# Local attention: score products over whole images, sorted into strips by TensorE

## The reference

```python
patches = extract_patches(x)                  # 25 shifts, 5x5, zero padding of 2
p = patches.reshape(N, NHEADS, hdim, K2, H, W)
q = x.reshape(N, NHEADS, hdim, 1, H, W)
scores = (p * q).sum(axis=2, keepdims=True)
att = jax.nn.softmax(scores, axis=3)
out = (p * att).sum(axis=3).reshape(N, D, H, W)
out = jnp.einsum('ndhw,od->nohw', out, w_out) + b_out[None, :, None, None]
```

## Time and profile before

| | us |
|---|---|
| median of three runs | 1821.26 |
| profiled execution | 1828.49 |
| its span | 1826.7 |
| PE / DVE / POOL / ACT busy | 1461.7 / 1532.3 / 1187.1 / 1052.0 |
| first half (window attention) | to about 799 |
| score products of head 0 on DVE | 819.4 to 883.3 |
| first subtraction of head 0, of head 7 | 888.6, 1647.3 |
| stores of the last halves | 1739.0 to 1753.7 |

### The profile page before, as it was taken

The page is one execution under the profiler, slowest core; times in us unless marked ns, Lnnn a source line. Parts: engine busy times, 40 slices in busy tenths (PEclk is TensorE's granted clock), DMA queues, the critical chain, the costliest instruction groups (busy, mean ns, idle before and its releaser), DMA issues.

```text
span 1826.7 us, 54921 instructions
## 1 busy us (share of the span) xinstructions
PE 1461.7 (80%) x22057; PEld 766.9 (42%) x22057; DVE 1532.3 (84%) x2231; ACT 1052.0 (58%) x1883; POOL 1187.1 (65%) x860
## 2 busy tenths in 40 slices
PE   5889999999999999946667877769687786867745
PEld 3667777777777777730122221212222122213322
DVE  5987777777777777769999999999989999896924
ACT  3567776666677777645454836667474665544300
POOL 4435554455444555410789899999999999996600
PEclk9999999999999999977789899999989999998878
DMA  8702010202014202032222225241332522117069
GB/s 331 271 14 53 18 53 18 53 18 53 13 48 81 53 18 53 18 108 60 61 50 70 59 50 127 50 110 32 72 92 50 126 50 50 26 44 278 21 266 403
DMA packets 106857, 156.07 MB, mean 85 GB/s; under 512 B 71362, under 2 KB 83650, under 8 KB 100034
## 3 DMA queue, kind: packets, MB, share of 16 engines
q1 hardware_dynamic: 106690, 153.60, 29.1%
HBM read 81.92 MB, written 65.20 MB: 81 GB/s over the span
## 4 chain that ended last, share of the span: by engine, by line
PE 37%; POOL 24%; DVE 18%; issue 13%; ACT 4%; SPq 1%; DVEq 1%; DMA 1%; POOLq 0%; ACTq 0%
POOL arena L801 18%; PE PS L1321 8%; PE PS L1309 6%; PE PS L1445 5%; PE PS L1275 4%; POOL arena L812 4%; PE PS L1300 4%; DVE arena L1213 3%; DVE arena L1104 3%; PE PS L1468 2%; DVE arena L1100 2%; PE PS L1279 2%; DVE consts L1152 2%; PE PS L1393 2%; DVE arena L1186 2%
## 5 line engine op out<-in xcount | busy, mean ns | idle before, releaser
L801 POOL TENSOR_TENSOR arena<-arena 128x2016 f32<-128x2016 f32 (+2 forms) x168 | 605.9, 3658 | 85.6 <-PE PS L1393 85.6
L1213 DVE TENSOR_TENSOR arena<-arena,PS 128x1568 f32<-128x1568 f32 x348 | 610.1, 1778 | 37.3 <-PE PS L1445 31.7
L1445 PE MATMUL PS<-arena,consts 32*32 32x392 f32 x12800 | 390.6, 512 | 101.5 <-DVE arena L1213 66.8
L767 POOL TENSOR_TENSOR arena<-arena,consts 128x196 f32<-128x196 f32 x512 | 294.7, 612 | 159.7 <-ACT arena L851 159.7
L992 ACT ACTIVATE PS<-arena 128x392 f32<-128x392 f32 x348 | 173.0, 499 | 281.9 <-DVE arena L1213 279.5
L1393 PE MATMUL PS<-arena,consts 128*32 128x504 f32 (+2 forms) x1664 | 222.7, 610 | 111.5 <-POOL arena L801 65.2
L1445 PEld LDWEIGHTS PS<-arena,consts 32*32 32x32 f32 x12800 | 137.5, 104 | 356.8 <-DVE arena L1213 206.0
L1321 PE MATMUL PS<-arena 128*128 128x96 f32 x2048 | 265.0, 272 | 3.5 <-ACT arena L864 2.0
L1321 PEld LDWEIGHTS PS<-arena 128*128 128x128 f32 x2048 | 249.1, 192 | 6.1 <-issue 3.9
L774 POOL TENSOR_TENSOR arena<-arena 128x392 f32 (+1 forms) x64 | 78.4, 1225 | 254.5 <-DVE arena L1131 254.5
L876 ACT ACTIVATE arena<-PS 128x512 f32<-128x512 f32 x256 | 151.8, 593 | 105.5 <-PE PS L1309 105.5
(11 more groups left out here) (105 smaller groups left out, 1693.5 us busy)
## 6 DMA issues: line engine op xcount, KB each, us to landing
arena<-x_wide_dram SPq DMA_DIRECT2D x256, 82.5 KB, 2.1
arena<-x_wide_dram SPq DMA_DIRECT2D x32, 660.0 KB, 8.1
x_wide_dram<-arena SPq DMA_DIRECT2D x12, 1125.0 KB
arena<-in_x_dram SPq DMA_DIRECT2D x8, 1568.0 KB, 14.9
x_wide_dram<-arena SPq DMA_DIRECT2D x64, 196.0 KB, 4.8
x_dram<-arena SPq DMA_DIRECT2D x8, 1568.0 KB, 7.7
attn_dram<-arena SPq DMA_DIRECT2D x256, 49.0 KB, 3.0
arena<-x_dram SPq DMA_DIRECT2D x8, 1568.0 KB, 18.1
```

The costliest lines, as they stand in the source:

```text
L767: i = nc.gpsimd.tensor_tensor(k_bd[k][:, r], keys.unsqueeze(1).to_broadcast([P, HEADS_T, S]), head_mask.unsqueeze(2).to_broadcast([P, HEAD ...
L801: nc.gpsimd.tensor_tensor(tile, x_part, by, ALU.mult).then_inc(pool_tile, 1)
L1213: nc.vector.tensor_tensor(by_channel(v_tiles[n % V_RING]), shifted_values(half, k), over_channels(PS[:, 2 + n % W_BANKS, 0:PIX]), ALU.mult ...
L1445: mm = nc.tensor.matmul(PS[dst, 4 + i, 0:PIX], ident[src, src], tile[src, c * PIX:(c + 1) * PIX], start=done == 0, stop=done == NK - 1)
```

## The change

- **Pixels for scores by whole images.** Two buffers `xs_maps` of 56 + 2 rows replace the four. A partition holds one channel of one image (8 channels x 16 images = 128), so one tile covers four strips of all images, `a` being odd or even strips. Products start at the strip's own rows: each row is multiplied once, and every tile has 4 x 7 x 56 = 1568 columns. The two rows below an image are zero.
- **Strips sorted by TensorE.** With a selection of 0 and 1 at stride 2 (`images`), `sum_scores` puts the sum of a strip on its partition, at columns from dy x 56 on. Its last dy rows go also to the next strip's partition, at columns from 0: up to four more matmuls of dy x 56 columns. Strip partitions are now numbered two per image within a group of 32 (`value_sel`, `load_for_values`, `store_half`).
- **DMAs.** The score loads of a head become 4 (were 32), those of its values 64 (were 4), its stores 64 (were 32).
- **Buffers and shares.** Rings of four instead of three (`S_RING`, `V_RING`); eight value products of a head on POOL instead of five; other places for reciprocal and scales.
- **Normalising.** Four steps of 784 pixels for a head's scores, and no clearing of halo rows for them. Small selections are made by POOL and DVE, and the parameters of the score channels by a product and a reduction instead of sixteen copies.

```diff
-TILE = CH * (GR + R) * W
+GROUPS = 4
+TILE = GROUPS * PIX
-S_RING, V_RING = 3, 3
+S_RING, V_RING = 4, 4
-RECIPROCAL_AT = 24
-SCALE_AT = [1, 3]
-SHARE_AT = [[9, 13], [18, 21, 24]]
-POOL_SHARE = [[(16, 18), (17, 21, 22)]] * (LH - 1) + [[range(18, NK), range(15, NK)]]
+RECIPROCAL_AT = 23
+SCALE_AT = [2, 4]
+SHARE_AT = [[8, 10, 12, 14], [17, 19, 21, 23]]
+POOL_SHARE = [[(11, 13, 16, 18), (13, 17, 21, 22)]] * (LH - 1) + [[range(18, NK), range(15, NK)]]
...
-                add("pe", ("sum", ("score", j, t, a)), 0.2 + 1.67e-3 * rows * cols,
+                add("pe", ("sum", ("score", j, t, a)), 0.85 + (0.1 + 0.095 * t_dy(t) if t_dy(t) else 0),
...
-        xs_halves = [room(GROUPS * HALO).rearrange("p (g h w) -> p g h w", g=GROUPS, h=HR) for _ in range(4)]
+        xs_maps = [room(IMAGE + R * WP).rearrange("p (h w) -> p h w", w=WP) for _ in range(2)]
         sc = [room(NK * PIX).rearrange("p (k n) -> p k n", k=NK)]
         early_pairs = used[1] // HW
...
-            r0, rows = R - dy, GR + dy
-            X = xs_halves[s_buf(j, a)]
-            here, there = X[:, :, r0:r0 + rows, R:R + W], X[:, :, R:R + rows, R + dx:R + dx + W]
+            X = xs_maps[j % 2]
+            def strips(down, right):
+                first = X[:, GR * a + down, R + right:R + right + 1]
+                return bass.AP(first.tensor, first.offset, [list(first.ap[0]), [2 * GR * WP, GROUPS], [WP, GR], [1, W]])
+            here, there = strips(0, 0), strips(dy, dx)
...
-            def load_for_scores(j, a, g, loaded):
-                for c in range(CH):
-                    src = bass.AP(at.tensor, at.offset, [[STRIP, GROUP], [1, HALO]])
+            def load_for_scores(j, half, loaded):
+                for b2 in range(2):
+                    src = bass.AP(at.tensor, at.offset, [[LINE, HD], [IMAGE, Q], [1, IMAGE]])
...
             def load_for_values(j, a):
-                for b2 in range(2):
-                    src = bass.AP(at.tensor, at.offset, [[STRIP, C], [LINE, CH], [1, HALO]])
+                for i in range(GROUPS):
+                    for b2 in range(2):
+                        for c in range(CH):
+                            src = bass.AP(at.tensor, at.offset, [[IMAGE, BP], [STRIP, 2], [1, HALO]])
...
                 for i in range(GROUPS):
                     for c in range(CH):
-                        sp.dma_start(dst[first:first + GROUP], o_loc[half][c * GROUP:(c + 1) * GROUP, i]).then_inc(o_stored[half], 16)
+                        for b2 in range(2):
+                            dst = attn_dram[b2, j * HD + half * CH + c, :, 2 * i:2 * i + 2]
+                            first = c * GROUP + b2 * 2 * BP
+                            src = o_loc[half][first:first + 2 * BP, i]
+                            sp.dma_start(dst, src).then_inc(o_stored[half], 16)
...
+            nc.vector.tensor_reduce(fold, ident.rearrange("p (c r) -> p r c", c=GROUPS), AX_X, ALU.add)
...
             for u in range(UNITS - 3, UNITS):
                 dve.wait_ge(added, u + 1)
                 unit_stats(u)
...
-            for g in range(GROUPS):
-                for c in range(CH):
-                    nc.vector.tensor_copy(par_s[c * GROUP:(c + 1) * GROUP, :, :, g], src[:, :, :, c])
...
+                i = nc.vector.tensor_tensor(par_of_all[:, n * P:(n + 1) * P].rearrange("p (j b c) -> p j b c", b=2, c=HD),
...
+            nc.vector.tensor_reduce(par_s, par_of_all.rearrange("p (n j c) -> p n j c", n=2, c=2 * HD), AX_X,
+                                    ALU.add).then_inc(score_par_ready, 1)
...
-                    mm = nc.tensor.matmul(PS[g * GROUP:(g + 1) * GROUP, 0, 0:rows * cols], fold,
-                                          tile[:, g * rows * cols:(g + 1) * rows * cols], start=a == 0, stop=a == 1)
+                    mm = nc.tensor.matmul(PS[block, 0, above:above + PIX], into, strip, start=a == 0,
+                                           stop=a == 1 and (g == 0 or above == 0))
+                if above:
+                    for g in range(GROUPS - a):
+                        block = slice((g + a) * GROUP, (g + a + 1) * GROUP)
+                        mm = nc.tensor.matmul(PS[block, 0, 0:above], into_next, tile[:, (g + 1) * PIX - above:(g + 1) * PIX],
+                                              start=False, stop=a == 1)
                 mm.then_inc(ring_summed, 1)
```

More of the change, by code:

```diff
@@ L195, in merge_orders @@
         if kind == "score":
-            rows, cols = shape_of(step[2])
-            columns = GROUPS * rows * cols
-            after = [freed, ("pixels", "s", j, step[3], GROUPS + 1)]
+            columns = TILE
+            after = [freed, ("pixels", "s", j, 0, pieces_of("s", j) - 1)]
             if n < 2 * S_TILES:
@@ L258, in merge_orders @@
         if kind == "s":
-            free = [("score", j - 2, S_TILES - 1, a)] if j >= 2 else []
+            free = [("score", j - 2, S_TILES - 1, 1), ("score", j - 2, SQUARE, 1)] if j >= 2 else []
         else:
             free = [s for s in V_ORDER + RING_ORDER if s[:3] == ("value", j - 1, a)]
-        for piece in range(GROUPS + 2):
-            add("act", ("pixels", kind, j, a, piece), 0.9 if piece < GROUPS else 0.7,
+        for piece in range(pieces_of(kind, j)):
+            add("act", ("pixels", kind, j, a, piece), 1.1 if kind == "s" else 0.9 if piece < CH else 0.7,
                 free + [("pixels", kind, j, a, piece - 1) if piece else None],
@@ L285, in merge_orders @@
     for kind, j, a in LATER:
-        free = [("score", j - 2, S_TILES - 1, a)] if kind == "s" else [s for s in V_ORDER + RING_ORDER if s[:3] == ("value", j - 1, a)]
+        free = [("score", j - 2, S_TILES - 1, 1), ("score", j - 2, SQUARE, 1)] if kind == "s" else [s for s in V_ORDER + RING_ORDER if s[:3] == ("value", j - 1, a)]
         sync.append((max(end[s] for s in free), ("load", kind, j, a)))
@@ L290, in merge_orders @@
              for j in range(LH) for half in range(2)]
-    sync.append((max(end[("score", LH - 1, S_TILES - 1, 1)], end[("total", LH - 2, NK - 1)],
+    sync.append((max(end[("score", LH - 1, S_TILES - 1, 1)], end[("score", LH - 1, SQUARE, 1)], end[("total", LH - 2, NK - 1)],
                      end[("weight", V_AT[("value", LH - 1, 0, 0)] - 1)]),
@@ L350, in build @@
         g_rstd, g_bias = g_pair[:, 0:BP], g_pair[:, BP:2 * BP]
-        row_sel = const(2 * 64)
-        edge_ones = const(2 * 16)
+        score_sel, value_sel = (const(2 * P).rearrange("p (n q) -> p n q", n=2) for _ in range(2))
         edge = const(2)
@@ L383, in build @@
         ring = [room(TILE) for _ in range(S_RING)]
+        v_tiles = [room(CH * PIX) for _ in range(V_RING)]
         xv = room(HD * HALO).rearrange("p (c h w) -> p c h w", c=HD, h=HR)
         sc.append(room(NK * PIX).rearrange("p (k n) -> p k n", k=NK))
-        v_tiles = [room(CH * PIX) for _ in range(V_RING)]
         lden_of_rows = room(GROUPS * PIX).rearrange("p (i n) -> p i n", i=GROUPS)
@@ L610, in load @@
             def load(kind, j, a):
                 if kind == "s":
-                    await_scores_made(sp, j - 2, a)
-                    for g in GROUP_ORDER:
-                        load_for_scores(j, a, g, xs_loaded)
+                    await_scores_made(sp, j - 2)
+                    for half in range(2):
+                        load_for_scores(j, half, xs_loaded)
                 else:
@@ L647, in _ @@
             for j in range(2):
-                for a in range(2):
-                    for g in GROUP_ORDER[:EARLY]:
-                        load_for_scores(j, a, g, xs_early)
+                load_for_scores(j, 0, xs_early)
             for bp in range(BP // 2 + 1, BP):
@@ L673, in reload_early @@
             def reload_early():
-                for a in range(2):
-                    await_scores_made(sp, LH - 1, a)
+                await_scores_made(sp, LH - 1)
                 sp.wait_ge(total_done, LH - 1)
@@ new lines, in normalise_pixels @@
+                if kind == "s":
+                    X, rows = xs_maps[j % 2], slice(piece % PARTS * 2 * GR, (piece % PARTS + 1) * 2 * GR)
+                    part = slice(0, P) if j >= 2 else slice(piece // PARTS * C, (piece // PARTS + 1) * C)
+                    if piece == 0 and j < 2:
+                        act.wait_ge(xs_early[j], 32)
+                        nc.scalar.activation(X[:, H:], no_rows.rearrange("p (h w) -> p h w", w=WP), ACT.Copy)
+                    elif piece % PARTS == 0:
+                        act.wait_ge(xs_loaded[j % 2], 32 + 64 * (j // 2))
+                    pixels = X[part, rows, R:R + W]
+                    i = nc.scalar.activation(pixels, pixels, ACT.Identity, bias=par_s[part, 1, j:j + 1], scale=par_s[part, 0, j:j + 1])
+                    if piece == pieces_of(kind, j) - 1:
+                        i.then_inc(xs_ready[j % 2], 1)
+                    return
@@ L929, in normalise_pixels @@
+                X = xv[:, a * CH:(a + 1) * CH]
+                if piece < CH:
+                    if piece == 0:
+                        if j == 0:
```

(7 more changed lines are left out.)

176 lines of the change are left out of this document (90 added, 86 removed).

## The result

The changed kernel takes 1860.59 us (1858.39 to 1861.52, four runs), the kernel before 1821.14 beside it: ratio 1.0215, interval 1.02 to 1.023. I had forecast 1793 in 1776 to 1822. The change makes the kernel 39 us slower.

What follows compares the result with a forecast made beforehand. Four limits in turn: POOL with DVE close behind in six heads, DVE first, a store gap, DMA bandwidth last. Terms -39.8 - 7.1 + 1 - 1.5 + 14.7 + 3.9 = -28.8 from 1828.5, less 7.2: 1793 us, range 1776 to 1822.

Steps and rivals of the forecast that it cites:

- SP's queue: In the heads, 148 DMAs for 84, most at 0.52, fill 80 of 103 us; ten us of slack, so 0.
- Rival (b): SP becomes the bound: 148 DMAs at 0.72 take 107 us, heads 106.6, 18 us more, total 1811; chance 0.13.
- Stores at the end: After the last scale, 64 uncovered stores instead of 32, at 0.459 each: +14.7 us, ends 5 and +20.
- the 7.2 taken off: Whole kernel: 7.2 us subtracted because the profiled execution (1828.5) lay above the median unprofiled time (1821.3).
- Rival (a): DVE's first maximum of each head loses the port to POOL: 48 us more if every head, total 1841; chance 0.11.
- POOL's heads: Heads 1 to 7: shorter vertical tiles at 3.15 us, POOL busy 102.1, a head 103.0 for 108.3; sum -39.8.
- Rival (d): Vertical tiles in the heads not shortened, 3.6 us each: POOL 111 us a head, total 1833; chance 0.03.
- Head 0: First head, on DVE: twenty of its 26 score products get shorter, at 1.78 us each: -7.1 us.
- The start: Before the heads: small selector operations +0.6 and the late image load; +1 us, ends 0 and 4.
- TensorE: Score tiles in the heads: eight short extra matmuls add 0.15 us per vertical tile, 3 us a head, covered.
- Last head: Late second-half values, six us of lateness covered, one more value buffer helping DVE: -1.5 us, ends -6 and +8.
- Final stage: DMA-bound end: early room holds five images, not six, so one more reload of 1568 KB: +3.9 us.

Runs made afterwards that it cites:

- e4: Kernel before with each store of 32 partitions split into two of 16 contiguous rows, 64 stores a head: 1836.64 us, one run.
- e12: Changed kernel with DVE's first maximum given one SBUF input, and each value load and store over 16 consecutive strips (wrong strip order, timing only): 1794.36 us, ratio 0.9841.
- e5: Changed kernel with one edit: DVE first copies the first score map into PSUM, so its first maximum has one SBUF input: 1849.31 us, ratio 1.0152.
- e7: Kernel before with one edit: DVE copies the first score map into PSUM, so its first maximum has one SBUF input: 1820.09 us, ratio 0.9995.
- e1: Changed kernel with value loads and stores merged into half as many DMAs of another pattern, 84 DMAs a head: 1813.47 us, ratio 0.9957.
- e6: Changed kernel with value loads and stores merged into half as many DMAs, and the first maximum given one SBUF input: 1783.29 us, ratio 0.9783.
- e2: Changed kernel with only the stores merged, 32 a head instead of 64: 1825.16 us, one run.
- e3: Changed kernel with only the value loads merged, 32 a head instead of 64: 1824.47 us, one run.
- e8: Changed kernel with value loads and stores merged and the score ring back at three, value ring at four: 1802.16 us, one run.

## Why the prediction was wrong

**The step that failed is "SP's queue"**, with its sentences "0.52 is the nearest" and "Ten us of slack: 0". The nearest row by kind was a load over 32 partitions; the DMA's pattern was another, and e4 and e12 show that the pattern decides. The trace of before even held a DMA in two dimensions, the value load at 0.62 (its row stands with e12), and the step did not use it. At the 104.0 us measured the slack is gone. From the end of a head's scores in after (t = 0 at 1311.13; the next two rows, of 1386.15 and 1398.60, stand in the section on the result):

```profile
1311.13 2.71 SPq L601 DMA_DIRECT2D arena<-x_wide_dram  x4
...
1318.80 23.19 SPq L613 DMA_DIRECT2D arena<-x_wide_dram  x32
1342.03 44.02 SPq L644 DMA_DIRECT2D attn_dram<-arena  x64
```

The second half's values are issued by t = 31 (forecast 19), the stores by 75 (52), the spread by 87 (64), the first half's values by 110 (81). ScalarE was ready for them at 100 and started at 112 (the wait of 11.22 before 1422.72, shown with e5 to e7). So what the step said would then follow did: ScalarE waits for the first half's values, with the weights behind it, and DVE follows. Rival (b) had 0.72 for all and 107 us of queue, close to the 104; its conclusion was "heads 106.6", and they are 108.4 to 110.1, because SP also waits between its groups. But I gave it 0.13 since "loads and stores cost 0.52 to 0.54". The spread's 0.72 on the earlier trace rows, which came close, was kept as an end of the range only; that it is close is in part luck, since a spread has another pattern again. Rival (b) also counted five of the six later heads; with six its price is 22 instead of 18.

**"Stores at the end" failed by the same price.** 64 x 0.459 = 29.4 was forecast, 42.7 measured, and the stated end of +20 was passed too: +28. ("0.6 each" would have been 64 x 0.6 - 14.7 = +24.) Rival (b) priced 0.72 in the heads and not here; carried through, 64 x (0.72 - 0.459) = 16.7 more, it would have come to 1828: slower.

Of the 67.6 us between 1793 and 1860.6, the heads make 45.6, the last stores 13.3 and the 7.2 taken off nearly all the rest.

**Rival (a) holds as well.** It gave 48 more over the heads if every head were hit. In after two of seven are hit; e1, where nothing hides it, has four long heads of seven, 40 us above e6. It named the mechanism, the ring that lets POOL hold on, and the first maximum. What was wrong is that (a) and (b) stood as exclusive cases with 0.11 and 0.13. They do not exclude each other: both come from the change, and both happened. In after they overlap: taking away the port gives 15.5 there and taking away the long queue 12.5, where each gives 40 and 37 once the other is gone.

**Right by the runs:**
- POOL's heads. The tile of 1568 columns with its operands apart costs about what I took between 2.86 and 3.60. After, POOL's forms from 820 us on:

```profile
L799 POOL TENSOR_TENSOR arena<-arena 128x1568 f32<-128x1568 f32 x168 | 517.5, 3113 | 74.8 <-PE PS L1424 71.7 <-PE PS L1429 2.7 <-PE PS L1481 0.3
```

  3.11 over the 24 tiles of a head, forecast (20 x 3.15 + 4 x 2.86) / 24 = 3.10. Rival (d) falls. The heads of e6 sum to 712.0: 46.7 less than the profiled execution of before, where the forecast said 39.8, and 35.4 less than e7, the kernel before with the same maximum.
- Head 0. From the first product to the first subtraction 61.4 for 69.2: -7.8, forecast -7.1. The start cost +2.7, not +1: the first product is at 822.12 for 819.42, and ScalarE's first piece of whole images at 813.34, where before the first piece started at 810.16. ScalarE then took its pieces without a pause, so the late image load was in time, and no run here shows it delayed by eight engines.
- TensorE. The eight short matmuls add little. One tile of after:

```profile
1178.06 0.87 PE L1424 MATMUL PS<-arena,consts 128*32 128x392 f32 x8
1178.75 0.28 PE L1429 MATMUL PS<-arena,consts 128*32 128x56 f32 x8
```

  1.0 in all, about +0.1 against the earlier trace rows, and TensorE is busy 82 to 85 of a head as it was.
- Last head, -2.1 for -1.5, by luck: the second half's values came so late that ScalarE waited 18.5 us for them, where the forecast had six us, all covered, and e1 shows 7.2 that SP's queue held there. The forecast met the sum and not its parts.
- Final stage, +5.3 for +3.9: one more reload, as forecast.

**The 7.2 us taken off.** The forecast took 7.2 off for a profiled execution that lay above its median. In after the two agree. The first maximum of head 1 took 11.05 in that execution of before, and in e4, which has the same maxima, 0.75, with a first distance of 104.9 for 114.4 (e7, 104.5). So the chance event that I took for a fixed part of the kernel may be most of the 7.2; no run shows it for the same kernel, and it stays a likely reading.

**Still open.** Why long and short heads take turns in e1 (heads 1, 3, 5 and 7); why the waiting DVE gets in at POOL's next boundary in some heads and is passed by in others; why no long maximum came in the one run with a ring of three and merged DMAs; and whether the second dimension or the eight makes a DMA dear to issue.

## What to carry to other kernels

- Price a DMA on its issuing queue by the pattern it will have, not by the nearest kind, and carry a price that a rival uses into every place where such DMAs are issued, the uncovered end above all. Here 148 DMAs at 0.7 were a head long, and at some 0.55 they cost the heads nothing (e12, 712.3 against 712.0 with half as many).
- Two rivals that come from the same edit can happen together. Ask for their joint time before giving chances; here each alone hid behind the other, and a two by two of experiments showed that both together are worth more than their sum (52.5 us in the heads for 12.5 and 15.5).
- Next to a dense stream of GpSimd products, let no operation of DVE on the path read two SBUF operands: in e6 a copy into PSUM and the two maxima behind it, one input in PSUM each, took 1.84 us together.

## What the runs showed of the hardware

- **Issue cost by pattern.** On SP: 0.46 to 0.57 for 16 rows in one dimension, 0.67 to 0.71 for eight by two, with the same bytes (rows shown of e12 and after; over all groups of a head up to 0.61 and 0.74). At the end of the kernels stores of eight images by four strips, twice the bytes, take 0.71 each (e6, 22.62 / 32), those by two 0.67 (after, 42.69 / 64).
- **A DVE operation can be passed by again and again.** Up to 16.4 us (e1, head 5). I followed up the first maxima of heads 1 to 7 in before, after, e1, e2, e3 and e8, 42 in all. Each ends 0.43 or 0.44 us after the end of a POOL operation. 29 got in behind the operation that was running when they started (0.76 to 3.60 us). The other 13 (9.72 to 16.42 us) were passed by at three to five boundaries and ended only once POOL had stopped, for 5.6 to 6.3 us, because its tiles had not been summed. None got in at a second or third boundary. The Trainium skill ("SBUF — State Buffer", who interferes with whom) has the loser blocked for the whole instruction of the other; that holds for one instruction (1.49), but here DVE waited through four to six.
- **A copy from SBUF into PSUM beside POOL's stream** took 0.56 in every head of e5, e6 and e7, against 0.75 to 16.4 for the maximum with two SBUF inputs in heads 1 to 7 (0.75 in e4, 16.4 in e1).
